# Layer 0 attention of a two-layer gated network: SyncE's order of stores and readbacks, and ScalarE's place for two copies

## The reference, cut to what matters

```python
q = ln @ Wq + bq                               # ln: normalised x, (8, 512, 256)
kv_input = jnp.concatenate([xn, ln], axis=1)   # (8, 1024, 256)
k, v = jnp.split(kv_input @ Wkv + bkv, 2, axis=-1)
sim = jnp.einsum('bhid,bhjd->bhij', q * DH ** (-0.5), k)
attn = jax.nn.softmax(sim, axis=-1)            # per head 512 x 1024
out = jnp.einsum('bhij,bhjd->bhid', attn, v)
x = x + jnp.tanh(g_xattn[0]) * (out @ Wo + bo)
```

## Time and profile before

| | us |
|---|---|
| median of 3 runs | 3198.53 (3198.34 to 3201.55) |
| the profiled execution | 3193.79 |
| its span, first to last instruction | 3192.2 |
| layer 0 attention within it | about the first 1660 |
| TensorE busy over the whole span | 2886.7 (90%) |
| VectorE, ScalarE, GpSimd busy | 2186.2, 1789.1, 1705.2 |
| mean granted TensorE clock | 0.951 |

### The profile page before, as it was taken

How to read it: one execution, slowest core, us unless ns; L and a number is a source line. 1 busy time by engine, 2 the same in 40 slices (tenths; PEclk the granted TensorE clock), 3 DMA queues, 4 the chain that set the end, 5 groups by cost and what they waited for, 6 DMA issues and landing times. The chain is left out here.

```text
span 3192.2 us, 46707 instructions
## 1 busy us (share of the span) xinstructions
PE 2886.7 (90%) x17032; PEld 2333.8 (73%) x17032; DVE 2186.2 (68%) x3482; ACT 1789.1 (56%) x2774; POOL 1705.2 (53%) x1054
## 2 busy tenths in 40 slices
PE   6899989899898999989977977999999976999999
PEld 5777777777777777777867974555555445999999
DVE  6667667676676767667664546777777735578887
ACT  4454444454554445445444534888888853366665
POOL 3443444334444344353324433888888762558886
PEclk9999999999999999999998987999999988999999
DMA  5653223242232423323235635433343214368885
GB/s 159 194 167 111 96 91 121 83 138 90 96 109 89 130 88 109 114 89 102 89 115 182 229 127 161 121 117 118 118 118 102 71 35 133 105 175 232 229 232 149
DMA packets 295880, 409.73 MB, mean 128 GB/s; under 512 B 30323, under 2 KB 216850, under 8 KB 295664
## 3 DMA queue, kind: packets, MB, share of 16 engines
q1 hardware_dynamic: 274864, 375.28, 36.7%
q0 software_dynamic: 18656, 29.00, 4.6%
q10 hardware_dynamic: 2144, 2.62, 0.2%
HBM read 259.51 MB, written 149.04 MB: 128 GB/s over the span
## 5 line engine op out<-in xcount | busy, mean ns | idle before, releaser
L1769 POOL TENSOR_TENSOR c_pT_lo<-c_prob,c_pT_hi 128x1024 fp32r<-128x1024 f32 x192 | 456.3, 2383 | 113.6 <-ACT c_pT_hi L1852 109.7
L484 ACT ACTIVATE a_prob<-a_scores,a_neg_max 128x1024 f32<-128x1024 f32 x256 | 285.8, 1116 | 336.9 <-DVE a_neg_max L600 336.9
L409 POOL TENSOR_TENSOR a_pT_lo<-a_turned,a_pT_hi 128x1024 fp32r<-128x1024 f32 x64 | 152.9, 2389 | 433.7 <-ACT a_pT_hi L476 433.5
L1964 DVE TENSOR_REDUCE c_neg_max<-c_max 128x2 f32<-128x1024 f32 x248 | 302.2, 1219 | 70.0 <-PE c_max L2197 68.9
L600 DVE TENSOR_REDUCE a_neg_max<-a_scores 128x1 f32<-128x1024 f32 x256 | 309.7, 1210 | 25.7 <-PE a_scores L36 24.5
L409 POOL TENSOR_TENSOR a_pT_lo<-a_prob,a_pT_hi 128x1024 fp32r<-128x1024 f32 x64 | 152.3, 2380 | 301.0 <-ACT a_pT_hi L476 301.0
L1846 ACT ACTIVATE c_prob<-c_scores 128x1024 f32<-128x1024 f32 x256 | 261.3, 1021 | 70.8 <-PE c_scores L2208 66.5
L34 PE MATMUL a_pj<-a_wv_hi,a_kvT_hi 128*128 128x256 f32 x512 | 159.0, 311 | 123.1 <-DVE a_v_lo L537 120.9
L34 PE MATMUL m_h<-m_rT_hi,m_w_hi 128*128 128x256 f32 x880 | 253.3, 288 | 1.9 <-DVE m_rT_lo L2698 1.9
L35 PE MATMUL m_h<-m_rT_lo,m_w_hi 128*128 128x256 f32 x880 | 248.4, 282 | 0.0
L36 PE MATMUL m_h<-m_rT_hi,m_w_lo 128*128 128x256 f32 x880 | 248.4, 282 | 0.0
(11 more groups left out here) (353 smaller groups left out, 9268.7 us busy)
## 6 DMA issues: line engine op xcount, KB each, us to landing
m_w_in<-L_ffn_w_in SPq DMA_DIRECT2D x117, 512.0 KB, 5.3
blocks_dram<-a_turned SPq DMA_DIRECT2D x64, 512.0 KB, 2.6
a_turned<-blocks_dram SPq DMA_DIRECT2D x256, 128.0 KB, 2.9
blocks_dram<-a_prob SPq DMA_DIRECT2D x64, 512.0 KB, 3.5
a_prob<-blocks_dram SPq DMA_DIRECT2D x256, 128.0 KB, 2.9
e_w_in<-L_ffn_w_in SPq DMA_DIRECT2D x32, 1024.0 KB, 7.5
qk_dram<-c_stage SPq DMA_DIRECT2D x64, 256.0 KB, 3.5
c_q_rows<-qk_dram SPq DMA_DIRECT2D x32, 512.0 KB, 4.8
```

The lines of the kernel that those rows point to most:

```text
L409: g.tensor_tensor(by_query(pT[1], t), from_blocks(staged[t]), by_query(pT[0], t).bitcast(F32), ALU.subtract).then_inc(turned_lo, 1)
L484: a(prob[:, qt, :], ps_s[:, qt % 2, :], ACT.Exp, bias=neg_max[:, qt:qt + 1], accum_out=row_sum[:, par, qt:qt + 1]).then_inc(exp_done, 1)
L1769: g.tensor_tensor(flat(pT[1][:, kt - 1]), flat(prob[:, kt]), flat(pT[0][:, kt - 1]).bitcast(F32), ALU.subtract).then_inc(lo_pool, 1)
L1964: ve.tensor_reduce(two, max_bank(n, qt)[:], AX.X, ALU.max, negate=True).then_inc(max_done, 1)
```

## The change

SyncE stores both turned tiles first, then reads both back, then loads the weights; for that the store and the readback become two functions, and the stores have a semaphore for each tile. In `plan`, `hi0` moves from behind `fin1` to a later place: behind `v0` in even steps, behind `qk2` in most odd ones. `hi1` moves behind `v2` in even steps. `zt1` moves ahead of `scores1`. The other edits only write `TILES` for 2 or make a wait name its own tile's count.

```diff
-        turned_out = sem("turned_out")
+        turned_out = [sem("turned_out_even"), sem("turned_out_odd")]
+        TILES = 2
             if par == 0:
-                steps = "scores0 turn3 qk0 qk1 scores1 tr0 fin0 tr1 scores2 fin1 hi0 scores3 qk2 v0 v1 hi1 v2 out0 turn2 v3 out1"
+                steps = "scores0 turn3 qk0 qk1 scores1 tr0 fin0 tr1 scores2 fin1 scores3 qk2 v0 hi0 v1 v2 hi1 out0 turn2 v3 out1"
             elif hp == 1 and b:
-                steps = "scores0 turn3 qk0 zt0 scores1 tr0 fin0 tr1 scores2 fin1 hi0 zt1 scores3 lg0 qk1 qk2 out0 turn2 hi1 out1"
+                steps = "scores0 turn3 qk0 zt0 zt1 scores1 tr0 fin0 tr1 scores2 fin1 scores3 lg0 qk1 qk2 hi0 out0 turn2 hi1 out1"
             elif hp == 2 and b:
-                steps = "scores0 turn3 qk0 scores1 tr0 fin0 tr1 scores2 fin1 hi0 cn0 scores3 qk1 qk2 out0 turn2 hi1 out1"
+                steps = "scores0 turn3 qk0 scores1 tr0 fin0 tr1 scores2 fin1 cn0 scores3 qk1 qk2 hi0 out0 turn2 hi1 out1"
             elif hp < 3:
-                steps = "scores0 turn3 qk0 scores1 tr0 fin0 tr1 scores2 fin1 hi0 scores3 qk1 qk2 out0 turn2 hi1 out1"
+                steps = "scores0 turn3 qk0 scores1 tr0 fin0 tr1 scores2 fin1 scores3 qk1 qk2 hi0 out0 turn2 hi1 out1"
             elif b < B - 1:
-                steps = "scores0 turn3 pro2 scores1 pro3 scores2 pro0 tr0 fin0 tr1 scores3 fin1 qk0 pro1 hi0 qk2 out0 qk1 turn2 hi1 out1"
+                steps = "scores0 turn3 pro2 scores1 pro3 scores2 pro0 tr0 fin0 tr1 scores3 fin1 qk0 pro1 qk2 out0 hi0 qk1 turn2 hi1 out1"
             else:
-                steps = "scores0 turn3 scores1 tr0 fin0 tr1 scores2 fin1 hi0 scores3 out0 turn2 hi1 out1"
+                steps = "scores0 turn3 scores1 tr0 fin0 tr1 scores2 fin1 scores3 hi0 out0 turn2 hi1 out1"
...
+            def write_blocks(n, t):
+                sp.wait_ge(block_turned, TILES * n + t + 1)
+                dma(blocks_dram[t], turned[:] if t == 0 else prob[:, 0, :]).then_inc(turned_out[t % 2], 16)
+
             def regroup(n, t):
-                sp.wait_ge(block_turned, 2 * n + t + 1)
-                dma(blocks_dram[t], turned[:] if t == 0 else prob[:, 0, :]).then_inc(turned_out, 16)
-                sp.wait_ge(turned_out, 32 * n + 16 * t + 16)
+                sp.wait_ge(turned_out[t], 16 * n + 16)
                 rows = blocks_dram[t].rearrange("(a i) (c f) -> c i a f", a=4, c=4)
                 for c in range(4):
                     dma(staged[t][32 * c:32 * c + 32].rearrange("i (a f) -> i a f", a=4), rows[c]).then_inc(turned_back[t], 16)

             def step(b, hp, par):
                 n, h = 8 * b + 2 * hp + par, (2 * hp + par + 4) % H0
+                write_blocks(n, 0)
+                write_blocks(n, 1)
                 regroup(n, 0)
+                regroup(n, 1)
                 if n + 4 < 8 * B:
                     sp.wait_ge(w_split, n + 3)
                     load_w(n + 4, h, par)
-                regroup(n, 1)
```

More of the change, by code:

```diff
@@ L407, in low @@
             def low(n, t):
-                pool.wait_ge(turned_hi, 2 * n + t + 1)
+                pool.wait_ge(turned_hi, TILES * n + t + 1)
                 g.tensor_tensor(by_query(pT[1], t), from_blocks(staged[t]), by_query(pT[0], t).bitcast(F32), ALU.subtract).then_inc(turned_lo, 1)
@@ L482, in exp @@
                 elif n and qt == 1:
-                    act.wait_ge(turned_lo, 2 * n)
+                    act.wait_ge(turned_lo, TILES * (n - 1) + qt + 1)
                 a(prob[:, qt, :], ps_s[:, qt % 2, :], ACT.Exp, bias=neg_max[:, qt:qt + 1],
@@ L590, in turn_blocks @@
                 if t == 0 and n:
-                    dve.wait_ge(turned_lo, 2 * n - 1)
+                    dve.wait_ge(turned_lo, TILES * (n - 1) + 1)
                 elif t == 1:
-                    dve.wait_ge(block_turned, 2 * n + 1)
+                    dve.wait_ge(block_turned, TILES * n + 1)
                 out = turned[:] if t == 0 else prob[:, 0, :]
@@ L760, in finish @@
                     pe.wait_ge(pj_out, TURNED[n, 3])
-                    pe.wait_ge(turned_lo, 2 * n + 2)
+                    pe.wait_ge(turned_lo, TILES * n + TILES)
                 for kt in range(4 * part, 4 * part + 4):
```

## The result

| | before | changed |
|---|---|---|
| median | 3198.44 (3192.93 to 3201.55, 4 runs) | 2998.31 (2997.18 to 3000.29, 4 runs) |
| ratio | | 0.9377 (95%: 0.936 to 0.9393) |
| profiled execution | 3193.79 | 3000.29 |

The account below looks back on a forecast made before the run. TensorE was taken to bound layer 0's attention, so only its idle time and clock could give. Gains of 118 + 45 + 13 + 4 + 2 = 182 us from 3193.79, plus 4.7 for the median, gave 3017 us; range 3000 to 3066.

Parts of the forecast that it names:

- Waits: TensorE's idle time in layer 0's attention: gains of 118 us for `a_v_lo`, 13 for `a_kT_lo`, 4 for `a_zero`.
- Clock: TensorE's half-clock stretches in layer 0's attention: 15 x 1.5 + 12 x 1.9 = 45 us gained.
- the six stretches behind the router: Half-clock stretches on TensorE following the small matmuls that score the router; expected to remain, no gain counted.
- the 27 stretches: Half-clock stretches on TensorE, counted at or just behind the end of `v3` waits; expected to go, worth 45 us.
- Tail: End of the attention stage: the 1.8 us wait for `a_pT_lo` goes, tile 1 being earlier; counted as 2 us.
- Rival 1: Readback of tile 0 lands 3 us later by queue order; 42 us of waits remain in even steps: 3059, chance 0.15.
- Rival 2: TensorE's waits go, but short groups still make the clock fall; the 45 us stay: 3062, chance 0.12.
- Rivals 3 and 4: 3: `v2` stays late through ScalarE's work or exponentials, 3180, chance 0.05; 4: late tile 0 lengthens even-step waits, 3247, chance 0.05.
- Rival 4: Tile 0 over about 6 us later, `hi0` holding `v1` and `v2`: slower, 3247 at 7.5 us, chance 0.05.
- all of the clock and no residual: Case given for the lower end, 3001, of the forecast's own range 3001 to 3034.
- the 3 us left over: TensorE's remaining wait before `v3`: 0.1 us left in each even step, taken off the 120.9 us.

## Why the prediction was right or wrong, point by point

**The mechanism held.** The wait for `a_v_lo` at `v3` went, as did ScalarE's wait for the second tile, store 1 leaves 0.03 us behind the turning, and no wait for `a_v_lo` that is left is longer than 0.7 us. Taking either order back brings 51 to 58 us of idle time back (66.0 and 72.5 against 14.7).

**The size: 182 us forecast, 193.5 us by the profiled executions.** The predicted 3017 lies 18.7 us above the measured 2998.31, which is 1.7 us below the range. By terms:

- Waits, 118 + 13 + 4 = 135 us: measured 133.5. In part that is luck: `a_v_lo` gave 112.3 of its 118, as 8.6 us of it came back before the turning, and small waits that the sum left out (3.6 us for `x_acc`, `a_kT_lo` and `a_v_lo` at other places) filled the gap.
- Clock, 45 us: TensorE's busy time fell by 63.8. **This is the step that failed**, mis-sized by 18.8 us. I left the six stretches behind the router out because their cause seemed untouched, while I moved `zt1` myself in a later paragraph and counted only its 4 us of waiting. The trace splits the 63.8 us. I take for each matmul the time to the next one's start, without idle time, and compare it with the mean of its shape in the changed kernel (0.235 us for 512 columns, 0.121 for 256). In the 27 stretches that I had counted, the matmuls took 45.0 us more than that, just what the prediction said. In the six behind the router they took 10.3 us more, which I had at nothing.
- The other 8.5 us of busy time lie outside the stretches, at full clock; the sum had no term for them. Most of it is how the profile counts a wait: the last matmul before one is counted with its whole length, 0.27 us for a turning of 128 columns, where otherwise the next starts 0.11 us behind it, and there are 38 waits fewer (70 to 32).
- By the Trainium skill (TensorE: Matmul & The Clock Gate, Terms) the 27 stretches were worth 66 us; for all 33, 157 us long, the same rule gives an estimate of 78. Measured in them are 55.3. The rule is too high here for the reasons that the rows show: TensorE is idle in some 31 of the 157 us, and of its busy time there 44% is lost, not 50.
- Tail, 2 us: measured -3.8. The wait for `a_pT_lo` went, but one of 1.5 us took its place, and another grew. The growth belongs to that execution alone: when the changed kernel ran again, the program took 1547.1 us from its last score matmul to the end, against 1547.0 before the change and 1550.8 in the first profile. So the tail gave about nothing.
- 18.8 - 1.5 - 5.8 = 11.5 us, which is 193.5 less 182. The other 7 us of the miss are the executions and rounding: the profiled one lay 4.7 us below the median before, which I carried over, and 2.0 above it after.

**Rival 1** (tile 0 late by the queue order): didn't occur, but it came nearer than I had worked out. I had tile 0 some 0.5 us later, at most 0.8; it came 1.2 us later, and the later place of `hi0` covered that. In all 64 steps the first quarter of readback 0 landed behind store 1, by 0.86 us in the median; it took 3.30 us from issue to landing where it had taken 2.55, so store 1 cost it 0.7 us and not its own 2.9. The Trainium skill (DMA: Bandwidth & Descriptors, Queues, rings and completion order) says that each engine consumes descriptors in ring order; the trace agrees with that order. **Rival 2** (the clock falls all the same): the stretches went from 33 to 0, not to 6. **Rivals 3 and 4**: not seen. Rival 4's place, `hi0` ahead of `v1` and `v2`, does decide when tile 0 is late by several microseconds (the run with the weights first), but even that run is 5% faster than the kernel before.

**The range.** Its lower end, 3000, had no room for a gain that I had called untouched; the upper side got 49 us, for rivals that never came. The 3001 given for "all of the clock and no residual" doesn't follow from the prediction's own figures either: with the 66 us in place of 45 and without the 3 us left over it would be 2993. One of the 27 stretches, the first, stands behind a wait of 2.23 us for `a_kT_lo` and not for `v3`; that changes nothing in the sum.

## What to carry to other kernels

When one in-order engine copies both from psum and from tiles that come by DMA, make the transfer early and put its consumer late: here each alone gave a little over half of the gain, and left waits at the next copies in the list. List the half-clock stretches with what stands just before each, and hold every edit against that list, the small ones too. And a saving on the bound engine that changes nothing by itself may be real, but absorbed by a chain that sets the pace; try it again when that chain is gone.

## What the runs showed of the hardware that I had not expected

At the end of the stage TensorE waits for VectorE, 3.52 us in the kernel before:

```profile
1651.67 1.82 PE L814 MATMUL a_pj<-k_ident,a_prob 128*128 128x128 f32 x8 [3.52 <-DVE x_acc L569]
```

and 5.71 us in the changed one, here with VectorE and GpSimd just before:

```profile
1450.24 2.35 POOL L414 TENSOR_TENSOR a_pT_lo<-a_turned,a_pT_hi 128x1024 fp32r<-128x1024 f32 x1 [14.29 <-ACT a_pT_hi L481]
1450.29 2.33 DVE L1220 TENSOR_SCALAR r_loc<-r_loc 128x4 f32<-128x4 f32 x1
...
1453.25 2.37 POOL L414 TENSOR_TENSOR a_pT_lo<-a_prob,a_pT_hi 128x1024 fp32r<-128x1024 f32 x1 [0.66 <-ACT a_pT_hi L481]
1453.33 2.32 DVE L1229 COPY r_sums<-r_sums 128x16 f32<-128x16 f32 x1
...
1456.58 1.94 PE L819 MATMUL a_pj<-k_ident,a_prob 128*128 128x128 f32 x8 [5.71 <-DVE x_acc L574]
```

All executions of line 1220 in the changed kernel (duration in ns, least, median, most):

```profile
L1220 DVE TENSOR_SCALAR r_loc<-r_loc x8: 169/170/2334, 374.4 to 1490.0; 128x4 f32<-128x4 f32 x8
```

Four numbers in each partition take 0.17 us, but 2.33 where GpSimd's subtraction began 0.05 us earlier, and both end within 0.03 us; the copy of line 1229 does the same 3 us later. It looks like a price of the new places of `hi0` and `hi1`, and it isn't. The kernel before has one such operation too, another line of the same group beside the same subtraction of GpSimd, which began at 1647.28:

```profile
1647.37 2.29 DVE L1209 TENSOR_TENSOR r_row_i<-r_row,r_off 128x4 int32<-128x4 f32 x1
```

And when the changed kernel ran again, lines 1220 and 1229 took 0.17 us each there and only line 1222 stood beside GpSimd's operation; TensorE waited as long as in the kernel before:

```profile
1451.29 2.21 DVE L1222 SCALAR_TENSOR_TENSOR route_row<-r_best,r_loc 128x4 int32<-128x4 f32 x1
...
1455.11 1.94 PE L819 MATMUL a_pj<-k_ident,a_prob 128*128 128x128 f32 x8 [3.44 <-DVE x_acc L574]
```

All twelve profiles of this document have such a long operation at this place (1.6 to 2.3 us, on one line or another of the group); the first one of the changed kernel alone has two, and its wait is 2.2 us longer. The Trainium skill (SBUF — State Buffer, SBUF: two separate sides) has the rule: VectorE and GpSimd share a port pair as an exclusive lock, which VectorE needs for a two-port mode or for two inputs in SBUF, and the one that comes second is blocked for the whole instruction. The rows agree with it. VectorE's operations with an input in psum took their usual time beside GpSimd's, for instance two of `a_pT_lo<-a_pj,a_pT_hi` in 1.28 us. The run that moved the router's operations found one of them (1.62 us) beside GpSimd's again and gained nothing.
